# Splitting q and k into fp16 parts, transposing them by DMA, and moving the scores to the start of a turn in a decoder layer

## The reference

```python
q = (x @ w_q.T); k = (x @ w_k.T); v = (x @ w_v.T)          # per sequence, split into 16 heads
q, k = rope(q), rope(k)                                    # x * cos + rotate_every_two(x) * sin
scores = where(causal, einsum("bhqd,bhkd->bhqk", q, k), -1e9) / sqrt(64)
x = layernorm(x + (softmax(scores) @ v) @ w_out.T)
sim = cosine similarity of ctx with its neighbours on the left and right
x = layernorm(x + conv3(x, weighted by sim))               # three taps over the channels
x = layernorm(x + bitlinear(silu(bitlinear(x, w_gate)) * bitlinear(x, w_up), w_down))
```

## Time and profile before

| | |
|---|---|
| median of three runs | 1351.74 us |
| the profiled execution's own time | 1352.4 us |
| span of its profile | 1350.6 us |
| mean granted clock of TensorE | 0.997 |
| PE / DVE / ACT / POOL busy | 98% / 77% / 48% / 17% |
| turns 6 to 13, first transpose of q | 355.02, then 405.23, 455.96, 505.70, 556.11, 605.86, 655.70, 705.67 us; turn 14 at 756.03, turn 15 at 795.35 |
| turns 3 to 6, first transpose of q | 205.99, 255.66, 305.35, 355.02 us |

### The profile page before, as it was taken

The page is one execution under the profiler, slowest core; times in us unless marked ns, Lnnn a source line. Parts: engine busy times, 40 slices in busy tenths (PEclk is TensorE's granted clock), DMA queues, the critical chain, the costliest instruction groups (busy, mean ns, idle before and its releaser), DMA issues. The chain is left out here.

```text
span 1350.6 us, 22488 instructions
## 1 busy us (share of the span) xinstructions
PE 1329.0 (98%) x7082; PEld 664.0 (49%) x7082; DVE 1036.5 (77%) x1857; ACT 648.3 (48%) x1241; POOL 233.3 (17%) x271
## 2 busy tenths in 40 slices
PE   8999999999999999999999999999999999999998
PEld 3455555545545545545545554444444444444443
DVE  5998456456488688688678777998888888888875
ACT  6888565465455355455455444333333333333321
POOL 0003222122221222221221230210000000000010
PEclk9999999999999999999999998999999999999999
DMA  9616644444434534434434586444444444444422
GB/s 377 248 43 189 214 146 157 168 137 168 168 112 155 178 110 163 169 114 163 165 115 170 162 247 178 104 115 120 107 108 113 107 107 107 107 114 114 110 49 68
DMA packets 127883, 194.75 MB, mean 144 GB/s; under 512 B 79409, under 2 KB 90849, under 8 KB 127841
## 3 DMA queue, kind: packets, MB, share of 16 engines
q1 hardware_dynamic: 127840, 194.22, 46.8%
HBM read 153.02 MB, written 25.43 MB: 132 GB/s over the span
## 5 line engine op out<-in xcount | busy, mean ns | idle before, releaser
L580 PE MATMUL ps<-weights,xT 128*128 128x512 f16 x2112 | 470.8, 379 | 1.7 <-DVE rope_s L1159 0.8
L580 PEld LDWEIGHTS ps<-weights,xT 128*128 128x128 f16 x2112 | 204.1, 98 | 236.5 <-issue 6.8
L826 PE MATMUL ps<-weights 128*128 128x512 fp8e4 (+1 forms) x1536 | 304.8, 358 | 1.3 <-DVE attn L1660 1.3
L826 PEld LDWEIGHTS ps<-weights 128*128 128x128 bf16 x1536 | 147.1, 98 | 158.3 <-issue 5.3
L1109 ACT ACTIVATE attn<-ps,xscale 128x512 f32<-128x512 f32 x96 | 61.5, 640 | 235.2 <-PE ps L826 235.1
L580 PE MATMUL ps<-weights 128*128 128x512 f16 x768 | 168.7, 379 | 0.0
L805 PE MATMUL ps<-weights 128*128 128x512 fp8e4 x704 | 154.4, 379 | 0.0
L856 ACT COPY attn<-ps 128x512 f32<-128x512 f32 x128 | 68.3, 585 | 156.5 <-PE ps L571 156.5
L924 ACT ACTIVATE attn<-attn,negmax,undo 128x128 f32<-128x128 f32 x256 | 122.7, 483 | 7.1 <-DVE negmax L1351 7.0
L580 PEld LDWEIGHTS ps<-weights 128*128 128x128 f16 x768 | 75.2, 98 | 89.4 <-DVE weights L1365 0.2
L805 PEld LDWEIGHTS ps<-weights 128*128 128x128 bf16 x704 | 68.6, 98 | 79.5
(11 more groups left out here) (169 smaller groups left out, 1681.9 us busy)
## 6 DMA issues: line engine op xcount, KB each, us to landing
wch<-w_ffn SPq DMA_DIRECT2D x96, 688.0 KB, 4.3
wch<-sim_scratch SPq DMA_DIRECT2D x96, 128.0 KB
ternary_scratch<-tern SPq DMA_DIRECT2D x48, 172.0 KB, 1.9
ctx<-ctx SPq DMA_DIRECT2D x16, 512.0 KB
wo_raw<-x_scratch SPq DMA_DIRECT2D x16, 512.0 KB, 4.7
x_in<-xT_in SPq DMA_DIRECT2D x15, 512.0 KB, 6.5
weights<-x SPq DMA_DIRECT2D x15, 512.0 KB, 10.4
x_scratch<-weights SPq DMA_DIRECT2D x15, 512.0 KB, 2.9
```

Source lines behind the costliest of these rows:

```text
L580: ins = nc.tensor.matmul(ps[:, bank], partsT[:, a, t], weights[:, t, w, half * HALF:(half + 1) * HALF], start=(t == 0 and a + w == 0), sto ...
L826: ins = nc.tensor.matmul(ps[:, 2 * w + a, 0:n], xqT[:, t], w8m[:, t, at:at + n], start=(t == 0), stop=(t == KT - 1))
```

## The change

From batch 2 on, rope's sum stays in rope_c. ACT casts it to a high fp16 part (qk_high_part), DVE subtracts that to get a low part (qk_low_part), both into the buffer of q. For each half of the heads one transposing DMA of 16 tiles of 128 x 128 on SP (load_qkT) brings the parts into qkT16. The scores of a head are then three fp16 products, and scores(0) comes first in a turn; qk_T and ACT's copies of its banks are gone. rope_add(b + 1, 3) moves ahead of x_all on POOL, mask_max(0) ahead of rope(b + 1, 0) on DVE. The last turn is put in another order, with one output half cut in two around prob_T(0). The diff, cut to what matters:

```diff
 qkT, prob, probT = (attn[:, j * D:(j + 1) * D].rearrange("p (w t n) -> p w t n", w=2, t=4) for j in (1, 2, 3))
+qk_parts = q[:].bitcast(F16).rearrange("p (m a n) -> p m a n", m=2, a=2)
+qkT16 = [buf.bitcast(F16).rearrange("p (m a t n) -> p m a t n", m=2, a=2, t=4) for buf in (attn[:, D:2 * D], k[:])]
 negmax = sb("negmax", [P, 2, 4], F32)
...
             sp.dma_start_transpose((hT_last if last else hT)[:, lo:hi], hq[:, lo * P:hi * P]).then_inc(hT_loaded[piece], 16)
+    def load_qkT(n, u):
+        sp.wait_ge(qk_low, qk_uses(n, 2 * u + 2))
+        sp.wait_ge(scores_full, n * 2)
+        if isinstance(n, int) and n == 2:
+            sp.wait_ge(tr_full[1], tr_pair(1, 1) + 1)
+        apart(sp)
+        sp.dma_start_transpose(qkT16[u].rearrange("p m a t n -> p (m a t) n"), qk_parts.rearrange("p m a n -> p (m a n)")) \
+            .then_inc(qkT_loaded[u], 16)
     def turn(b, mode, has_next, has_next2):
...
             sp.dma_start(xres_last, x[b + 1]).then_inc(xres_last_loaded, 16)
+            load_qkT(b + 1, 0)
             for w in range(2):
                 sp.wait_ge(pj_full[w], pj_uses(B - 1, 2 + w) + 1)
             load_w8(0, 0)
             load_w8(0, 4)
             load_w8(1, 0)
+            load_qkT(b + 1, 1)
             sp.wait_ge(weighed, 3)
             load_sims(1)
         if mode != "plain":
+            later = not (isinstance(b, int) and b == 0)
+            if later and not second:
+                load_qkT(b + 1, 0)
             for c in range(4 if second else 2, SUMS if mode == "sum" else CUTS):
+                if later and c == (5 if second else (SUMS if mode == "sum" else CUTS) - 1):
+                    load_qkT(b + 1, 1)
                 if mode == "cut":
...
         def scores(u):
+            if not (isinstance(b, int) and b < 2):
+                pe.wait_ge(qkT_loaded[u], (b - 1) * 16)
+                pe.wait_ge(scores_free, b * 4 + 2 * u)
+                for t in range(4):
+                    for a, w in ((0, 0), (0, 1), (1, 0)):
+                        for r in range(2):
+                            rows = slice(64 * r, 64 * r + 64)
+                            ins = nc.tensor.matmul(ps[:, SC + r, t * P:(t + 1) * P], qkT16[u][rows, 0, a, t],
+                                                   qkT16[u][rows, 1, w, t], start=(a + w == 0), stop=(a == 1))
+                ins.then_inc(scores_full, 1)
+                return
             for w in range(2):
...
             return
-        qk_T(0)
+        scores(0)
         proj(0)
         if isinstance(b, int) and b == PASS:
             pe.wait_ge(abs_done, 1)
             pe.wait_ge(oT_ready, b * 2)
             nc.tensor.matmul(ps[:, OB, 0:3], ones, abs_sum[:, 0:3], start=True, stop=True).then_inc(abs_summed, 1)
-        scores(0)
-        qk_T(1)
         proj(1)
...
         nc.scalar.copy(conv_parts[:, kk, 0], convG[:, kk + 1]).then_inc(conv_high, 1)
+    def qk_high_part(n, j):
+        act.wait_ge(roped, n * 4 + j + 1)
+        if j >= 2:
+            act.wait_ge(qkT_loaded[0], (n - 1) * 16)
+        elif isinstance(n, int) and n == 2:
+            act.wait_ge(tr_full[0], tr_pair(1, 1) + 1)
+        else:
+            act.wait_ge(qkT_loaded[1], (n - 2) * 16)
+        nc.scalar.copy(qk_parts[:, j % 2, 0], rope_c[:]).then_inc(qk_high, 1)
     def turn(b, mode, has_next, has_next2):
...
             return
-        for w in range(2):
-            copy_bank(w, tr_pair(b, 0), qkT[:, w])
-        act.wait_ge(scores_full, b * 2 + 1)
-        for w in range(2):
-            copy_bank(w, tr_pair(b, 1), qkT[:, w])
         exps(0)
+        qk_high_part(b + 1, 0)
         ctx_square()
         abs_chunk(0)
         sign_chunk(0)
         act.wait_ge(pv_full, b * 2)
         for w in range(2):
             copy_bank(w, tr_pair(b, 2), probT[:, w])
+        qk_high_part(b + 1, 1)
         exps(1)
...
             copy_bank(w, tr_pair(b, 3), probT[:, w])
+        qk_high_part(b + 1, 2)
         abs_chunk(4)
         abs_chunk(5)
         sign_chunk(2)
+        qk_high_part(b + 1, 3)
         prelude = has_next and not has_next2
...
             dve.wait_ge(pj_full[j % 2], pj_uses(n, j) + 1)
-        dve.wait_ge(roped, n * 4 + (j if at is None else at))
+        if (isinstance(n, int) and n == 1) or (isinstance(n, int) and n == 2 and j == 0):
+            dve.wait_ge(roped, n * 4 + (j if at is None else at))
+        else:
+            dve.wait_ge(qk_low, qk_uses(n, j))
         src = ps[:, OB + j // 2 if raw else PJ + j % 2]
...
             rope_sum((q, k)[j % 2][:, j // 2 * HALF:(j // 2 + 1) * HALF])
+    def qk_low_part(n, j):
+        dve.wait_ge(qk_high, qk_uses(n, j) + 1)
+        nc.vector.tensor_tensor(qk_parts[:, j % 2, 1], rope_c[:], qk_parts[:, j % 2, 0], ALU.subtract).then_inc(qk_low, 1)
     def power(dst, src):
...
         def turn_last():
+            mask_max(0)
             residual(0, PJ)
-            mask_max(0)
+            normalise(0)
             norm_sums(x2n)
-            normalise(0)
+            mask_max(1)
+            dve.wait_ge(xres_loaded, b * 16)
+            residual_half(b - 1, 0, OB, xres, undo_out[:, 0:1])
             norm_x(1)
             scale_x()
             move_xscale(0)
-            mask_max(1)
-            dve.wait_ge(xres_loaded, b * 16)
-            residual_half(b - 1, 0, OB, xres, undo_out[:, 0:1])
+            normalise(1)
             integers_x(0)
-            normalise(1)
             s = residual_half(b - 1, 1, OB, xres, undo_out[:, 0:1])
...
             threshold_sums()
+        mask_max(0)
         rope(b + 1, 0)
-        mask_max(0)
         if first_cut:
             thresholds()
         normalise(0)
         if prelude:
             dve.wait_ge(convw_in, 16)
             nc.vector.tensor_reduce(cfit[:, 0:1], convw, AX_X, ALU.max, apply_absolute_value=True).then_inc(conv_max, 1)
+        qk_low_part(b + 1, 0)
         rope(b + 1, 1)
         mask_max(1)
+        qk_low_part(b + 1, 1)
         ctx_norms()
...
         cut_chunk(1)
+        qk_low_part(b + 1, 2)
         rope(b + 1, 3)
...
         cut_chunk(2)
+        qk_low_part(b + 1, 3)
         if not prelude:
...
         pool.wait_ge(pj_free[j % 2], pj_uses(n, j) + 1)
-        pool.wait_ge(tr_full[j % 2], tr_pair(n - 1, j // 2) + 1)
-        nc.gpsimd.tensor_tensor((q, k)[j % 2][:, j // 2 * HALF:(j // 2 + 1) * HALF], rope_c[:], rope_s[:], ALU.add) \
-            .then_inc(roped, 1)
+        nc.gpsimd.tensor_tensor(rope_c[:], rope_c[:], rope_s[:], ALU.add).then_inc(roped, 1)
     def x_all(n):
...
             rope_add(b + 1, 2)
+        if has_next and not (isinstance(b, int) and b == 0):
+            rope_add(b + 1, 3)
         if has_next2 and not (isinstance(b, int) and b == 0):
             x_all(b + 2)
-        if has_next and not (isinstance(b, int) and b == 0):
-            rope_add(b + 1, 3)
         pool.wait_ge(dots_ready, b + 1)
```

More of the change, by code:

```diff
@@ L237, in decoder @@
         roped = sem("roped")
+        qk_high = sem("qk_high")
+        qk_low = sem("qk_low")
+        qkT_loaded = [sem("qkT_loaded0"), sem("qkT_loaded1")]
         scores_full = sem("scores_full")
@@ L301, in tr_pair, with qk_uses @@
         def tr_pair(b, j):
-            return b * 4 + j
+            if isinstance(b, int) and b < 2:
+                return b * 4 + j
+            return b * 2 + 4 + (j - 2)
+        def qk_uses(n, j):
+            return (n - 2) * 4 + j
         def pj_uses(n, j):
@@ L470, in turn @@
                     store_sims(0)
+                    load_qkT(2, 0)
                     w_load(2)
@@ L711, in turn @@
                     conv(0, PJ)
-                    scores(0)
-                    qk_T(1)
-                    out_proj(b - 1, 0, OB)
                     scores(1)
+                    pe.wait_ge(oT_ready, (b - 1) * 2 + 2)
+                    product(OB, oT, w_parts[:, 3], 0, tiles=range(KT // 2))
                     prob_T(0)
+                    product(OB, oT, w_parts[:, 3], 0, tiles=range(KT // 2, KT)).then_inc(pj_full[0], 1)
                     out_proj(b - 1, 1, OB)
@@ L982, in turn_second @@
                     exps(0)
+                    qk_high_part(2, 0)
                     abs_chunk(-4)
@@ L988, in turn_second @@
                     abs_chunk(-2)
+                    qk_high_part(2, 1)
                     exps(1)
@@ L992, in turn_second @@
                     abs_chunk(0)
+                    qk_high_part(2, 2)
                     oT_high_part(0)
@@ L997, in turn_second @@
                         copy_bank(w, tr_pair(1, 3), probT[:, w])
+                    qk_high_part(2, 3)
                     abs_chunk(2)
@@ L1341, in mask_max @@
                     dve.wait_ge(scores_full, b * 2 + (u + 1))
-                    dve.wait_ge(tr_full[1], b * 4 if u == 0 else tr_pair(b, 2) + 1)
+                    early = isinstance(b, int) and b < 2
+                    dve.wait_ge(tr_full[1], tr_pair(b, 0 if early else 2) if u == 0 else tr_pair(b, 2) + 1)
                     for r in range(2):
```

(4 more changed lines are left out.)

4 lines of the change are left out of this document (1 added, 3 removed).

## The result

The changed kernel takes 1409.99 us (median of five runs, 1406.58 to 1413.58) against 1351.74 for the kernel before: 1.0426 times as long, interval 1.041 to 1.0441. The profiled execution is the longest of the five, 1413.58, with a span of 1411.8, so its differences add up to 61.2 us of span and not to the 58 of the medians.

A forecast was written before the change was run, and what follows sets the result against it. PE (98% busy) and a closed loop through ctx and DVE were taken as balanced within a quarter microsecond. Cut turns 30, sum turns 5.6 and the end 5 gave 41 on 1352.4: 1392 us, range 1366 to 1410.

The forecast's parts named there:

- term A: Eight cut turns, b = 6 to 13: DVE's longer loop costs 3.8 us each, 30 in all.
- term B: Four steady sum turns, b = 2 to 5: transposes ahead of w_load(2) delay proj(5), 4 x 1.4 = 5.6 us.
- turn 1: Turn 1 was said to have slack for its small delays: 0 us.
- turns 14 and 15: Late rope_add(1) holds DVE in turn 14, the last turn gives some back: +5 us, between -4 and +10.
- The mechanism: Cut turns: qk_low(1) waits for a cast behind ctx, lengthening DVE's loop; PE's gain is lost waiting at pv(0).
- The loop through ctx: Cut turns: closed loop from first_norm through ctx's load and DVE to the next first_norm, about 49.75 us, 0.24 below the turn.
- The rival of the absorbed half: Cut turns lose only 2 us because cut_chunk(0) drops from 3.59 towards 1.65: 1372 us, chance 0.15.
- The price of a score: On PE, 24 fp16 matmuls per score taken as 1.1 us, between 0.67 and 1.63.
- that rival: PE's clock falls behind its idle time at pv(0) of cut turns, about 1.5 us in eight turns: 1404, chance 0.14.
- The faster rival: PE stays the bound and 14 turns gain 1.8 us each if ctx and the cast come earlier: 1327, chance 0.06.

The follow-up runs named there:

- e1: Changed kernel with ACT's cast qk_high_part(b+1, 1) moved ahead of ctx_square, b = 2 to 13; 1387.48 us, ratio 1.0269.
- e2: Changed kernel with SP issuing the load of ctx for the next turn at the end of the present one; 1360.83 us, ratio 1.0064.
- e3: Kernel before the change, with the load of ctx for the next turn issued at the end of the present one; 1348.53 us, ratio 0.9981.
- e5: Changed kernel, turn 14 alone: POOL's rope_add(15, 1) ahead of the all-reduce, DVE's convw_factors behind rope(15, 2); 1410.4 us, ratio 1.0443.
- e6: Changed kernel, turn 1 alone: cast qk_high_part(2, 1) behind ctx_square, subtraction qk_low_part(2, 1) behind the residual; 1411.62 us, ratio 1.0443.
- e9: Changed kernel with ctx loaded early, cut_chunk(3) ahead of x_factors, and sum turns, turn 1 and turn 14 reordered; 1326.02 us, ratio 0.9823.
- e7: Changed kernel with ctx loaded at the previous turn's end and, in cut turns, cut_chunk(3) ahead of x_factors; 1355.18 us, ratio 1.0015.

## Why the prediction was right, and where it was not

The forecast was 1392 within 1366 to 1410, and 0.89 for slower. 1409.99 is slower, as forecast, but lies inside the range by 0.01: two of the five runs are above it. That it lies inside is luck. The terms add up to 41, and the profiled execution shows 61: term A came out 3 smaller, term B 13 larger, turn 1 6 larger, and turns 14 and 15 nearly 5 larger.

- **The mechanism held.** The loop through ctx, the wait of qk_low(1) for a cast behind ctx, and the gain of PE lost at pv(0) are all in the trace: +3.2 where 3.3 was worked out, +0.7 for 0.62, +0.3 for 0.1 to 0.2, PE at 94%, waits of 3.18 and 1.66 where 3.5 and 1 to 2 were named. Cut turns gave +26.6 for the 30 of term A. The cast and the subtraction took 0.63 and 0.69 where halves of wider rows had given 0.52 and 0.62. e1 and e2 show the causes by taking them away, e3 that PE and loop were balanced. The rival of the absorbed half fell with its condition: cut_chunk(0) kept its 3.59.
- **The price of a score** was taken as 1.1 us, between 0.67 and 1.63; two scores cost 0.77 each from start to start (scores at 700.50, the projection behind at 701.27), so PE saves 2.5 us a turn and not 1.8. 24 matmuls one after the other are 1.33 at the 56 ns of the prediction, and 1.33 to 0.77 is 1.7 times. The Trainium skill (TensorEngine Tiling (Array Packing), Theoretical Speedup) puts the gain at up to twice, and this row stays below that. As the prediction said, it did not matter for the time in a cut turn.
- **The step that failed is term B**, "4 x 1.4 = 5.6", with 18.8 measured (14.2 and 12.7 in e5 and e6, with the same program in these turns). Its chain was right: transposes ahead of w_load(2), copy, cast, rope(3), proj(5). Its size was not. w_load(2) was 4.3 later into the turn than in the earlier trace rows, near the 4.8 forecast, but the copy for pv(1) came 33.2 into the turn and not 31.5, since abs_chunk(2) started 4.9 after w_load(2) was issued, and abs_chunk(3) 6.0 after abs_chunk(1) had freed its buffer, where I had used the median of 4.3: 1.5 us a turn. The other part, 1.4 to 1.7 a turn, was the clock in this execution. I had that rival and placed it at pv(0) of cut turns. There it came in six of eight, but at no price that can be seen, where 1.5 a turn was forecast; what it cost came at proj(5) of sum turns, and in turns 1 and 14.
- **Turn 1 was put at 0** and cost 6.3. I called its slack enough without following ACT: qk_high(2, 1) ahead of exps(1) delayed the residual and pv(0) by 2.5, half clock added 1.5, and v_chunk behind late loads 1.3. e6 shows that these three do not simply add: without the first, the last grew to 4.41, and the late loads alone still set the turn's end.
- **Turns 14 and 15 were put at 5** and cost 9.6, inside the bound of 10. rope_add(15, 1) came 26.8 into the turn, 2.1 later than in the earlier trace rows, because the weights of the convolution came later too; half clock added about 3.8 (0.9 in prob_T(1), 2.9 in proj(4)).
- **The faster rival**, 1327, named a condition that is needed but not enough: ctx and the cast come earlier. e2 makes that true and takes 1360.83; e9, with other moves as well, takes 1326. That its number agrees with 1327 is luck in part: PE saves 2.5 a turn and not 1.8, but e9 collects only 2.0 of it in a cut turn and 2.3 in a sum turn.

Not settled: which move would take the last of PE's waits out of the cut turns of e9 (about 0.3 before prob_T(0), for normalise, and 0.2 behind prob_T(1), for rope), and why the clock fell at proj(5) in one execution and not in another with the same waits.

## What to carry to other kernels

When an engine is 98% busy, look for a second closed loop of the same length before counting a saving on the first; here the place of one load decided between 58 us lost and 10. An instruction added in the middle of an in-order program costs what stands in front of its input on the other engine, not its own duration. Taking away one wait of several in a chain mostly moves it (e5, e6), so follow the chain to the next resource before pricing the repair. A fall of the clock costs time only where PE's product is on the chain that sets the turn. And before one profile of an edit is set against one profile of the kernel, look at how far two profiles of an unchanged part lie apart.

## What was not expected of the hardware

- A short wait can be followed by a loss as large as itself, and need not be. 1.56 us before proj(5) were followed by 1.69 us of slower product, at a granted clock of 0.57; the same 1.56 in e6 were followed by a product of 5.35. Among cut turns a wait of 3.70 was followed by 7.01, one of 3.18 by 5.35. In e9, where PE waits at most 0.6 us from turn 2 to turn 14, the clock did not fall there, and its mean over the execution was 0.998 against 0.978.
- An all-reduce on POOL holds the engine longer than its row says. In the cut turn of batch 12 x_maximum ended at 737.90, the row is at 744.09 with 0.38 us, and POOL's next instruction came at 751.57, though its input had been there since 741.6: 7.10 us of idle time in which it waited for nothing that the profile shows. In e2 and e7, where the load of ctx is issued about then, sum turns show 9.6 to 11.6 us in place of 7.1; the cause was not tried.
- DVE's 128x512 product in normalise took 2.88 us at 294.11, beside POOL's multiplication of ctx (294.08, 2.36), and 0.69 at 297.11 without it.
